# A two-layer graph network on one core: index tables kept in SBUF, a carry row fetched, vector features on ScalarE, a dense scale on GpSimd, four loads under way

## The chip, the cores and the metric

The kernel runs on one core of a Trainium2 chip. Its time is device microseconds (us) of one execution. The core's engines are TensorE (PE in the profile; PEld are its weight loads), VectorE (DVE), ScalarE (ACT), GpSimd (POOL) and SyncE (SP), and each works through its own queue of instructions in order. Semaphores tie the queues together.

## The reference

There are 100,000 nodes with 160 features (64 scalars, 32 vectors of three components) and 25,000 edges, sorted by destination. Two layers each normalise, send messages along the edges, sum them at the destination and add the result back:

```python
h = jnp.maximum(_layernorm(x), 0.0)
x = x + L0(h, node_vec1, edge_attr_4, edge_attr_8, ...)   # cos(angle) * self part + sin(angle) * edge part
h = jnp.maximum(_layernorm(x), 0.0)
x = x + L1(h, edge_attr_4, ...)                            # h + relu(linear(segment_sum(message)))
# L0, per edge, with gs, gv = linear(h)[src] and w1..w4 = silu(edge_attr_8 @ fc_w1) @ fc_w2:
m0a = gs * ys * w1;   m0b = sum(gv * yv, -1) * w4;   m1a = gs * yv * w2;   m1b = gv * ys * w3
mid = segment_sum([m0a, m0b, m1a, m1b], dst) / 4           # then two linear maps and the angle
```

A node without an incoming edge needs only its self part, and that is most of them.

## The kernel before, in words

Nodes are worked in 98 units of 1,024 (128 partitions by 8), edges in 196 tiles of 128, four tiles to a quad, so 49 quads (Q = 49, T = 196, GQ = 4). The program has four stages that follow one another.

**Head.** SP loads the tables of sources and destinations. DVE makes from them the gather index (`t_gat`), the scatter index (`t_put`: an edge that isn't the last of its destination gets an index out of range) and the keys `f_key` (own destination and that of the last edge before the tile). PE transposes the destinations into rows. SP stores all of these to DRAM by quad (lines 409 to 418). Then the edge network: for 13 groups of four quads, `net_load` brings the edge scalars, PE multiplies (`net_mm`, L1037), ACT applies SiLU (`net_silu`, L803), `net_store` writes the hidden values to DRAM.

**Stage 1** runs the dense part and the edge part of layer 0 together: 98 steps, each a unit of nodes and two tiles of edges (one half-step, or slot, for each tile). In a slot PE does the dense products of the unit before (`dense_mm`), transposes features of the tile before (`p1_feat_t`, L1090), then `p1_parts`, `p1_source` (the linear map of the gathered source rows and their weights, L1066), `p1_sum` (sum over equal destinations, L1078 and L1080) and `dense_tr` (L976). The sum and the dense transposes share PSUM bank 1, so `dense_tr` waits until ACT has copied the sum out (`p1_total`, L832, waited for as `e_tot`). ACT, in a slot: copy the transposed features (L838), the rest (L817), scale the source rows (`p1_source`, L824), copy the sum (L832), then the transposed dense rows (L795) and four layer-norm-and-relu instructions (`dense_h1`, L774). Two of the four slots of a quad differ: in one PE also transposes the next quad's edge rows, which ACT copies (L811) before PE may go on. DVE has the statistics, the dense residual (L1358), the features in three parts (L1423, L1428, L1432) and, each quad, two selector matrices (`selector`, L1384): `same` (edges of one destination) and `carry` (edges that continue the last destination of the tile before). POOL gathers the source rows by indirect DMA (`gather`, L606), makes scales, and adds `x1 + h1` (`dense_y`, L649).

**Stage 2** takes the destination rows again, quad by quad: POOL gathers four tiles (L606) and scatters four tiles of the layer's result (L612), index columns having been loaded by SP for each quad (`p2_index`, `p2_put`).

**Stage 3** is the edge part of layer 1, one tile to a slot. POOL alternates one scatter (L612) and one gather (L738), the gather seven tiles ahead. PE in slot n: transpose n-1, `p3_sum` n-4 (which waits for `m_sc`, the selectors), `p3_parts` n-2. DVE in slot n: features n, message n-2, output n-4, and in the last slot of a quad the selector `same` of the next quad (`p3_same`). SP, for each quad: `p3_load`, `p3_tables`, `p3_y`.

## Time and profile before

| | us |
|---|---|
| median of 3 runs (2452.57 to 2453.29) | 2452.86 |
| the profiled execution's own time | 2459.89 |
| its span, first to last instruction | 2458.1 |
| busy: PE / DVE / ACT / POOL | 1824.8 / 1873.4 / 1296.0 / 1477.5 |

The profiled execution is a single one, and took 7.0 us more than the median. Its span is what the views below divide up. Busy time is an average over four stages that differ, so a share of the whole says little about which engine a stage waits for.

### The profile page before, as it was taken

To read this page: it belongs to the slowest core of one execution; us is meant where nothing else is said; L and a number is where in the kernel's file an instruction comes from. 1 tells how busy PE (TensorE), PEld (TensorE's weight loads), DVE (VectorE), ACT (ScalarE), POOL (GpSimd) and SP (SyncE) were. 2 spreads that over 40 slices of the span, in tenths; PEclk is the share of its full clock that TensorE was granted. 3 is DMA by queue.
4 is the path that set the end of the run, shared out by engine and by line. 5 is a ranking of instruction groups with operands and counts; after the bars stand their busy time and mean duration, and the time that the engine had idled before them with its cause. 6 is when DMAs were issued, how large, how long until landed. Compare 5 with 4: busy or idle time off the path is not lost.

```text
span 2458.1 us, 51427 instructions
## 1 busy us (share of the span) xinstructions
PE 1824.8 (74%) x12730; PEld 1696.7 (69%) x12730; DVE 1873.4 (76%) x5982; ACT 1296.0 (53%) x3409; POOL 1477.5 (60%) x1432
## 2 busy tenths in 40 slices
PE   0788888888888888888888554544543788898887
PEld 0287778777787777877777544444443788888887
DVE  2099999999999999999999676666666566665564
ACT  0256666666666666666666555555555333333332
POOL 1045455554545555455553677777777777777776
PEclk9999999999999999999999755555555899998999
DMA  9445555555555555555555534334433334444443
GB/s 85 145 139 186 196 206 202 196 188 195 200 201 203 190 195 191 201 205 194 195 184 185 172 108 118 114 116 123 117 117 117 94 105 111 115 111 110 113 115 85
DMA packets 236558, 377.35 MB, mean 154 GB/s; under 512 B 116353, under 2 KB 146108, under 8 KB 236364
## 3 DMA queue, kind: packets, MB, share of 16 engines
q1 hardware_dynamic: 189484, 302.66, 39.1%
q0 software_dynamic: 47040, 74.31, 11.2%
q8 instruction: 12, 0.20, 0.0%
q14 instruction: 22, 0.18, 0.0%
HBM read 183.27 MB, written 201.21 MB: 156 GB/s over the span
## 4 chain that ended last, share of the span: by engine, by line
PE 33%; issue 17%; DVE 14%; ACT 12%; DMA 12%; POOL 6%; SPq 4%; ACTq 1%; DVEq 1%; POOLq 0%
ACT h L774 6%; PE bank L981 5%; DMA q_row<-row_tab 4%; PE bank L976 4%; DMA x_all<-in_xa,i_dst 3%; DVE st L1207 3%; POOL h_all L612 3%; PE bank L1090 3%; PE bank L982 3%; PE bank L1066 2%; DMA out<-yo,i_put 2%; POOL x_all L606 2%; PE bank L1158 2%; ACT h L889 2%; ACT tot L832 2%
## 5 line engine op out<-in xcount | busy, mean ns | idle before, releaser
L649 POOL TENSOR_TENSOR yo<-x,h 128x640 f32<-128x640 f32 x196 | 303.9, 1551 | 506.2 <-ACT h L774 504.9
L981 PE MATMUL bank<-wp,hT 128*128 128x160 f32 x1568 | 376.3, 322 | 0.0
L774 ACT ACTIVATE h<-x,nmr,inv 128x160 f32<-128x160 f32 x784 | 342.2, 514 | 1.5 <-DVE nmr L1211 1.5
L606 POOL DMA_INDIRECT x_e<-in_xa,i_src x192 | 210.8, 1098 | 161.1 <-issue 78.3
L981 PE MATMUL bank<-wp,eT 128*128 128x160 f32 x784 | 263.0, 428 | 51.2 <-ACT eR L897 43.7
L982 PE MATMUL bank<-wp,hR 128*128 128x64 f32 x1568 | 259.4, 247 | 0.0
L1358 DVE SCALAR_TENSOR_TENSOR x<-bank,scl,x_all 128x160 f32<-128x160 f32 x784 | 254.7, 365 | 5.1 <-PE bank L982 1.8
L982 PEld LDWEIGHTS bank<-wp,hR 128*128 128x128 f32 x1568 | 255.5, 190 | 0.0
L612 POOL DMA_INDIRECT out<-yo,i_put x196 | 209.7, 1070 | 74.3 <-issue 41.0
L612 POOL DMA_INDIRECT h_all<-h,i_put x196 | 217.4, 1109 | 59.8 <-issue 58.9
L976 PE MATMUL bank<-ident,h_e 128*128 128x128 f32 x392 | 83.9, 353 | 215.8 <-DVE hr_e L1527 215.4
L981 PEld LDWEIGHTS bank<-wp,hT 128*128 128x128 f32 x1568 | 237.7, 192 | 2.1
L738 POOL DMA_INDIRECT h<-h_all,i_src x196 | 200.2, 1022 | 61.5 <-issue 44.5
L606 POOL DMA_INDIRECT x_all<-in_xa,i_dst x196 | 192.4, 981 | 59.6 <-issue 57.8
L795 ACT ACTIVATE hT<-bank 128x512 f32<-128x512 f32 x196 | 117.0, 597 | 208.2 <-PE bank L977 208.2
L1207 DVE BATCH_NORM_STATS2 st<-x 128x6 f32<-128x320 f32 x490 | 217.9, 484 | 0.0
L976 PEld LDWEIGHTS bank<-ident,h_e 128*128 128x128 f32 x392 | 58.2, 185 | 224.7 <-DVE hr_e L1527 207.1
L981 PEld LDWEIGHTS bank<-wp,eT 128*128 128x128 f32 x784 | 163.5, 258 | 70.7 <-issue 38.2
L976 PE MATMUL bank<-ident,hb 128*128 128x128 f32 x784 | 124.3, 281 | 110.3 <-ACT tot L832 110.3
L946 ACT ACTIVATE tot<-bank 128x160 f32<-128x160 f32 x196 | 59.0, 301 | 267.9 <-PE bank L1181 264.0
L1158 PE MATMUL bank<-ident,feat 128*128 128x128 f32 x784 | 129.0, 290 | 93.2 <-DVE feat L1688 92.5
L976 PEld LDWEIGHTS bank<-ident,hb 128*128 128x128 f32 x784 | 83.1, 141 | 152.5 <-issue 137.6
(161 smaller groups left out, 5508.3 us busy)
## 6 DMA issues: line engine op xcount, KB each, us to landing
x_all<-in_xa SPq DMA_DIRECT2D x98, 644.0 KB, 5.0
h_all<-h SPq DMA_DIRECT2D x98, 640.0 KB, 3.0
out<-yo SPq DMA_DIRECT2D x98, 640.0 KB, 3.3
q_row<-row_tab SPq DMA_DIRECT2D x98, 256.0 KB
sum_tab<-tot SPq DMA_DIRECT2D x49, 322.0 KB, 4.2
y_tab<-yo SPq DMA_DIRECT2D x49, 320.0 KB
x<-y_tab SPq DMA_DIRECT2D x49, 320.0 KB
cv<-sum_tab SPq DMA_DIRECT2D x25, 322.0 KB, 3.2
```

The source lines that it names most:

```text
L606: nc.gpsimd.indirect_dma_start(into[:, t * width:(t + 1) * width], None, rows, bass.IndirectOffsetOnAxis(ap=index[:, t:t + 1], axis=0)).th ...
L612: nc.gpsimd.indirect_dma_start(rows, bass.IndirectOffsetOnAxis(ap=index[:, t:t + 1], axis=0), tile, None, bounds_check=N - 1, oob_is_err=F ...
L649: nc.gpsimd.tensor_tensor(yo[j][:, a:b], x1[j][:, a:b], h1[j][:, a:b], ALU.add).then_inc(d_y, 1)
L738: nc.gpsimd.indirect_dma_start(h1[j][:, t * D:(t + 1) * D], None, h1_all, bass.IndirectOffsetOnAxis(ap=i_src[j][:, t:t + 1], axis=0)).then ...
L774: ins = nc.scalar.activation(h1[j][:, k * D:(k + 1) * D], x1[j][:, k * D:(k + 1) * D], ACT.Relu, bias=nmr2[j][:, k:k + 1], scale=inv2[j][: ...
L795: nc.scalar.activation(hT[h][:, :], bank[0][:, :], ACT.Relu)
L976: nc.tensor.transpose(ps_main[:, t * P:(t + 1) * P], main[:, t * P:(t + 1) * P], ident[:, :])
L981: nc.tensor.matmul(dst_ps, main[:, t * P:(t + 1) * P], wp[:, w:w + D], start=True, stop=False)
L982: return nc.tensor.matmul(dst_ps[:, 0:DS], rest[:, :], wp[:, w + D + t * DS:w + D + (t + 1) * DS], start=False, stop=True)
L1158: ins = nc.tensor.transpose(bank[n.mod(2)][:, c * P:(c + 1) * P], feat[n.mod(2)][:, c * P:(c + 1) * P], ident[:, :])
L1207: return V.bn_stats(st[:, 2 * pair:2 * pair + 2, :].rearrange("p g k -> p (g k)"), two_rows[:, 0:D, :])
L1358: ins = V.scalar_tensor_tensor(x1[j][:, k * D:(k + 1) * D], bank[2 + pair % 2][:, k % 2 * D:(k % 2 + 1) * D], scl1[u.mod(4)][:, k:k + 1], ...
```

## The change

Five edits. (1) The index columns of a quad are copied on POOL from tables that stay in SBUF, into the small buffers that the indirect DMAs read. The four tables in DRAM, their stores and SP's loads of them go, and with them `q_key`; the selector `same` reads its keys from `f_dst` in SBUF, and the rows of destinations come from the host's transposed copy. (2) Of `carry` only the last partition holds anything: DVE makes all rows of it once in the head (`c_row`), they go to DRAM, and SP fetches one row for each quad into partition 127; the product that uses it contracts over 32 partitions. (3) The third part of the features (L1432) goes; ACT makes a second, scaled copy of the vector part of the source rows instead, three instructions of 32 columns for each tile, with a scale `scly` that POOL makes. (4) `dense_scale` moves from DVE to POOL. (5) The edge network has four loads under way, not two.

SP, head (stores that go) and the edge network:

```diff
-            sp.dma_start(src_tab.rearrange("q p c -> p q c"), t_src[:, :].rearrange("p (q c) -> p q c", c=GQ)).then_inc(s_tab_out, 16)
-            sp.dma_start(dst_tab.rearrange("q p c -> p q c"), t_gat[:, :].rearrange("p (q c) -> p q c", c=GQ)).then_inc(s_tab_out, 16)
-            sp.dma_start(put_tab.rearrange("q p c -> p q c"), t_put[:, :].rearrange("p (q c) -> p q c", c=GQ)).then_inc(s_tab_out, 16)
-            sp.dma_start(key_tab.rearrange("q p c -> p q c"), f_key[:, :, :]).then_inc(s_tab_out, 16)
...
-                wait(sp, n_mm, 2 * (g - 1))
...
+                wait(sp, n_mm, 2 * (g - 3))
...
-            net_load(0)
+            for g in range(4):
+                net_load(g)
+            sp.wait_ge(s_car, 1)
+            sp.dma_start(carry_tab[0:TA, :], c_row[0][0:TA, :]).then_inc(s_car_out, 16)
+            if T > P:
+                sp.dma_start(carry_tab[P:T, :], c_row[1][0:T - P, :]).then_inc(s_car_out, 16)
             for g in range(NB):
-                if g + 1 < NB:
-                    net_load(g + 1)
                 net_store(g)
+                if g + 4 < NB:
+                    net_load(g + 4)
```

SP's tables in stage 1, and in stage 3 (the waits come ahead of the loads):

```diff
             def p1_tables(q):
                 j = q.mod(2)
                 wait(sp, e_v, q.times(GQ, -GQ))
-                sp.dma_start(q_key[j][:, :], key_tab[q.times(1)]).then_inc(e_tb[j], 16)
                 sp.dma_start(q_ed[j][:, :], ed_q[q.times(1)]).then_inc(e_tb[j], 16)
                 sp.dma_start(q_row[j][:, :], row_q[q.times(1)].partition_broadcast(P)).then_inc(e_tb[j], 16)
+
+            def p1_carry(q):
+                j = q.mod(2)
+                wait(sp, e_seg, q.times(GQ, -GQ))
+                sp.dma_start(carry[j][P - 1:P, :], carry_q[q.times(1)].unsqueeze(0)).then_inc(e_ca[j], 16)
...
                 if v.within(U) and (v - 2).within(U):
                     x_load(v, last)
-                if v.mod(2) == 0 and (q + 1).within(Q):
-                    p1_load(q + 1)
+                if v.mod(2) == 0 and q.within(Q):
+                    p1_tables(q)
                 if v.mod(2) == 1 and q.within(Q):
-                    p1_tables(q)
+                    p1_carry(q)
                     p1_hidden(q)
...
             def p3_tables(q):
                 j = q.mod(2)
                 wait(sp, m_v, q.times(GQ, -GQ))
-                sp.dma_start(q_key[j][:, :], key_tab[q.times(1)]).then_inc(m_tb[j], 16)
+                wait(sp, m_seg, q.times(GQ, -GQ))
                 sp.dma_start(q_ed[j][:, :], ed_q[q.times(1)]).then_inc(m_tb[j], 16)
                 sp.dma_start(q_row[j][:, :], row_q[q.times(1)].partition_broadcast(P)).then_inc(m_tb[j], 16)
+                sp.dma_start(carry[j][P - 1:P, :], carry_q[q.times(1)].unsqueeze(0)).then_inc(m_tb[j], 16)
```

POOL:

```diff
+            for j in range(2):
+                nc.gpsimd.memset(carry[j][:, :], 0.0)
+            nc.gpsimd.memset(tot[1][:, :], 0.0).then_inc(s_cz, 1)
+
+            def index_copy(into, table, q, signal):
+                nc.gpsimd.tensor_copy(into[:, :], table[:, bass.ds(q.times(GQ), GQ)]).then_inc(signal, 1)
+                pool.wait_ge(signal, q.times(1, 1))
 
             def p1_gather(q):
                 j = q.mod(2)
-                pool.wait_ge(e_ix[j], q.over(2, 16, 16))
+                wait(pool, e_g[j], q.over(2, 64))
+                index_copy(i_src[j], t_src, q, e_ix)
                 wait(pool, e_cen, q.times(1, -1))
+                wait(pool, e_scl, q.times(4, -4))
                 gather(xa, x_e[j], XW, i_src[j], e_g[j])
...
+            def dense_scale(u):
+                j = u.mod(4)
+                pool.wait_ge(d_scl, u.times(2, 1))
+                nc.gpsimd.tensor_tensor(scl1[j][:, :], inv1[j][:, :], x3(x_in[j], XW, GD)[:, :, D], ALU.mult).then_inc(d_scl, 1)
...
+                pool.wait_ge(e_tb[j], q.over(2, 32, 32))
+                nc.gpsimd.tensor_tensor(scly[j][:, :].rearrange("p (t i) -> p t i", i=3), bc_last(scl_e[j][:, :], 3),
+                                        x3(q_ed[j], EW, GQ)[:, :, 1:4], ALU.mult).then_inc(e_scl, 1)
 
 
             def step(w):
                 q = At(w.i, w.c // 2, 2)
...
                 k = q.mod(4)
-                pool.wait_ge(r_ix[k], q.over(4, 16, 16))
+                wait(pool, r_g[k], q.over(4, 64))
+                index_copy(i_dst[k], t_gat, q, r_ix)
                 wait(pool, r_x1, q.times(2, -6))
                 gather(xa, x_q[k], XW, i_dst[k], r_g[k])
 
             def p2_scatter(q):
                 j = q.mod(2)
-                pool.wait_ge(r_px[j], q.over(2, 16, 16))
+                wait(pool, r_put[j], q.over(2, 64))
+                index_copy(i_put[j], t_put, q, r_px)
                 pool.wait_ge(r_h1, q.times(1, 1))
...
             def p3_gather(n):
                 j, t = n.c // GQ % 2, n.mod(4)
                 if t == 0:
-                    pool.wait_ge(m_ix[j], n.over(8, 16, 16))
+                    wait(pool, m_g[j], n.over(8, 64))
+                    index_copy(i_src[j], t_src, At(n.i, n.c // GQ, 2), m_ix)
...
                 if t == 0:
-                    pool.wait_ge(m_px[j], n.over(8, 16, 16))
+                    wait(pool, m_put[j], n.over(8, 64))
+                    index_copy(i_put[j], t_put, At(n.i, n.c // GQ, 2), m_px)
```

ACT in `p1_source`, PE in `p1_sum` and DVE's features and selector in stage 1:

```diff
+                act.wait_ge(e_scl, n.over(4, 4, 4))
                 wait(act, e_ft, n.times(1, -1))
-                nc.scalar.activation(g_e[n.mod(2)][:, :], bank[5 + n.mod(2)][:, 0:D], ACT.Copy,
-                                     scale=scl_e[j][:, t:t + 1]).then_inc(e_gg, 1)
+                g, b = g_e[n.mod(2)], bank[5 + n.mod(2)]
+                nc.scalar.activation(g[:, 0:D], b[:, 0:D], ACT.Copy, scale=scl_e[j][:, t:t + 1])
+                for c in range(3):
+                    ins = nc.scalar.activation(g[:, D + c:D + DV:3], b[:, DS + c:D:3], ACT.Copy,
+                                               scale=scly[j][:, 3 * t + c:3 * t + c + 1])
+                ins.then_inc(e_gg, 1)
...
-                before = tot[j][:, (t - 1) * CW:t * CW] if t else tot[1 - j][:, (GQ - 1) * CW:GQ * CW]
+                before = tot[j][P - 32:P, (t - 1) * CW:t * CW] if t else tot[1 - j][P - 32:P, (GQ - 1) * CW:GQ * CW]
                 nc.tensor.matmul(bank[1][:, U_SEG:U_SEG + CW], same[j][:, t * P:(t + 1) * P], v_e[n.mod(2)][:, :],
                                  start=True, stop=False)
-                nc.tensor.matmul(bank[1][:, U_SEG:U_SEG + CW], carry[j][:, t * P:(t + 1) * P], before,
+                nc.tensor.matmul(bank[1][:, U_SEG:U_SEG + CW], carry[j][P - 32:P, t * P:(t + 1) * P], before,
                                  start=False, stop=True).then_inc(e_seg, 1)
...
-                                       bc_last(q_key[j][:, key * GQ:(key + 1) * GQ], P), ALU.is_equal)
+            def selector(q):
+
+                j = q.mod(2)
+                key = f_dst[:, bass.ds(q.times(GQ), GQ)]
+                return V.tensor_tensor(x3(same[j], P, GQ), x3(q_row[j], P, GQ), bc_last(key, P), ALU.is_equal)
 
...
                     v.wait_ge(e_gg, n.times(1, 1))
                     wait(v, e_ftr, n.times(1, -1))
                     V.tensor_tensor(f[:, 128:320].rearrange("p (a u i) -> p a u i", a=2, i=3),
                                     w[:, 128:192].rearrange("p (a u) -> p a u", a=2).unsqueeze(3).to_broadcast([P, 2, DU, 3]),
-                                    g[:, DS:D].rearrange("p (u i) -> p u i", i=3).unsqueeze(1).to_broadcast([P, 2, DU, 3]),
-                                    ALU.mult).then_inc(e_fm, 1)
-                elif part == 1:
+                                    g[:, DS:D + DV].rearrange("p (a u i) -> p a u i", a=2, i=3), ALU.mult)
+                else:
                     V.tensor_tensor(f[:, 0:128].rearrange("p (a u) -> p a u", a=2), w[:, 0:128].rearrange("p (a u) -> p a u", a=2),
-                                    bc_mid(g[:, 0:DS], 2), ALU.mult)
-                else:
-                    v.wait_ge(e_fm, n.times(1, 1))
-                    V.tensor_tensor(f[:, 224:320].rearrange("p (u i) -> p u i", i=3),
-                                    f[:, 224:320].rearrange("p (u i) -> p u i", i=3),
-                                    bc_mid(ed(j, t, 1, 4), DU), ALU.mult).then_inc(e_ft, 1)
+                                    bc_mid(g[:, 0:DS], 2), ALU.mult).then_inc(e_ft, 1)
```

The order of instructions, at three places. POOL in the loop of stage 2, before: one gather of four tiles and one scatter of four, with SP's loads waited for.

```order
L72 ISA [waits p2_index_loaded0]
L606 DMA x_all<-in_xa,i_dst 128x161 [waits p2_x1_steps]
L606 DMA x_all<-in_xa,i_dst 128x161 x3
L703 ISA
L704 ISA [waits p2_put_loaded0]
L612 DMA h_all<-h,i_put 100000x160 [waits p2_h1_ready]
L612 DMA h_all<-h,i_put 100000x160 x3
L72 REGISTER_ALU [waits p2_index_loaded1]
L606 DMA x_all<-in_xa,i_dst 128x161 [waits p2_x1_steps]
L606 DMA x_all<-in_xa,i_dst 128x161 x3
```

The same place now (`i_dst` and `i_put` are the index columns of a quad):

```order
L620 ISA [waits p2_node_rows0]
L620 COPY i_dst<-t_gat 128x4
L621 ISA
L72 ISA [waits p2_index_copied]
L586 DMA x_all<-in_xa,i_dst 128x161 [waits p2_x1_steps]
L586 DMA x_all<-in_xa,i_dst 128x161 x3
L72 ISA
L620 ISA [waits p2_h1_scattered0]
L620 COPY i_put<-t_put 128x4
L621 ISA
L592 DMA h_all<-h,i_put 100000x160 [waits p2_put_copied,p2_h1_ready]
L592 DMA h_all<-h,i_put 100000x160 x3
```

Between two runs of four indirect DMAs there stands now a copy, and the DMA behind it waits for POOL's own copy.

ACT in a slot of stage 1, before:

```order
L817 ACTIVATE xr<-bank 128x65 [waits p1_message_ready]
L820 REGISTER_ALU
L822 ISA [waits p1_products_done]
L72 REGISTER_ALU [waits p1_scale_ready]
L824 ACTIVATE g_e<-bank,scl_e 128x160 [waits p1_features_ready]
L832 ACTIVATE tot<-bank 128x161 [waits p1_sum_done]
L72 ISA [waits dense_h_transposed]
L795 ACTIVATE hT<-bank 128x512 [waits dense_product_done]
L796 ACTIVATE hR<-bank 128x128
```

And now:

```order
L827 REGISTER_ALU [waits p1_products_done]
L72 REGISTER_ALU [waits p1_scale_ready]
L830 ACTIVATE g_e<-bank,scl_e 128x160 [waits p1_features_ready]
L832 ACTIVATE g_e<-bank,scly 128x32 x3
L841 ACTIVATE tot<-bank 128x161 [waits p1_sum_done]
L72 ISA [waits dense_h_transposed]
L800 ACTIVATE hT<-bank 128x512 [waits dense_product_done]
L801 ACTIVATE hR<-bank 128x128
```

Three more instructions stand between the source scale and the copy of the sum (`tot`), for which PE's next dense transposes wait.

SP in the loop of stage 3, one quad, before:

```order
L552 ISA [waits p3_h1_rows0]
L552 DMA i_src<-src_tab 128x4
L557 ISA [waits p3_message_ready]
L557 DMA q_key<-key_tab 128x8
L558 ISA
L558 DMA q_ed<-edges 128x24
L559 DMA q_row<-row_tab 128x512
L564 ISA [waits p3_out_ready]
L564 DMA x<-y_tab 128x640
L566 DMA i_put<-put_tab 128x4 [waits p3_out_scattered1]
```

And now:

```order
L542 ISA [waits p3_sum_done,p3_message_ready]
L542 DMA q_ed<-edges 128x24
L543 ISA
L543 DMA q_row<-row_tab 128x512
L544 DMA carry<-carry_tab 1x512
L549 ISA [waits p3_out_ready]
L549 DMA x<-y_tab 128x640
```

The load of the row tables waits now for `p3_sum_done` too, the sum of the last tile of the quad before, and the carry row is fetched last of three.

## Rows read from the trace of the kernel before

**Rows 1.** Stages 1 to 3: busy us of each engine, granted clock, DMA share.
```profile
core 0: us, PE busy (x) PEld busy (x) DVE busy (x) ACT busy (x) POOL busy (x), PEclk, DMA share, GB/s
118.00:1378.00 1260.00, 1049.75 (x8080) 987.84 (x8080) 1181.32 (x3324) 805.03 (x2251) 649.88 (x629) 1.00 0.55 193
1378.00:1908.00 530.00, 260.80 (x1029) 233.15 (x1029) 358.53 (x1523) 288.24 (x539) 408.87 (x392) 0.54 0.41 118
1908.00:2458.00 550.00, 464.99 (x3528) 457.70 (x3528) 319.06 (x1077) 184.19 (x588) 409.72 (x392) 0.93 0.40 107
```

**Rows 2.** Timeline of the head: start, length (us), engine, line, tile, idle before.
```profile
39.54 14.67 SPq L412 DMA_DIRECT2D key_tab<-f_key  x1
...
60.94 0.82 SPq L427 DMA_DIRECT2D yo<-scalars_t  x2
...
63.98 7.16 PE L1037 MATMUL bank<-yo,wp 32*128 32x512 f32 x8 [44.74 <-DMA yo<-scalars_t]
...
111.92 0.28 ACT L803 ACTIVATE x<-bank 128x128 f32<-128x128 f32 x1
```

**Rows 3.** DMA issues: the copy that the edge network waits for.
```profile
scalars_t<-in_scalars_t_in SPq DMA_DIRECT2D x1, 784.0 KB, 9.7
```

**Rows 4.** Timeline of PE in stage 1: the dense transposes of four slots.
```profile
603.50 0.63 PE L976 MATMUL bank<-ident,hb 128*128 128x128 f32 x4 [0.59 <-ACT tot L832]
...
609.18 0.63 PE L976 MATMUL bank<-ident,hb 128*128 128x128 f32 x4 [0.60 <-ACT tot L832]
...
615.92 0.63 PE L976 MATMUL bank<-ident,hb 128*128 128x128 f32 x4 [0.59 <-ACT tot L832]
...
623.37 0.63 PE L976 MATMUL bank<-ident,hb 128*128 128x128 f32 x4 [0.59 <-ACT tot L832]
```

**Rows 5.** Groups by line and shape: busy us, mean ns, idle before by releaser.
```profile
L795 ACT ACTIVATE hT<-bank 128x512 f32<-128x512 f32 x196 | 117.0, 597 | 208.2 <-PE bank L977 208.2
...
L1432 DVE TENSOR_TENSOR feat<-feat,q_ed 128x96 f32<-128x96 f32 x196 | 107.0, 546 | 0.0
...
L1090 PE MATMUL bank<-ident,feat 128*128 128x128 f32 x588 | 101.4, 282 | 87.5 <-ACT eR L812 47.3 <-DVE feat L1432 40.1
```

**Rows 6.** Timeline of ACT in stage 1, one slot.
```profile
608.08 0.39 ACT L824 ACTIVATE g_e<-bank,scl_e 128x160 f32<-128x160 f32 x1 [0.65 <-PE bank L1066]
608.62 0.30 ACT L832 ACTIVATE tot<-bank 128x161 f32<-128x161 f32 x1 [0.15 <-PE bank L1080]
...
610.69 1.75 ACT L774 ACTIVATE h<-x,nmr,inv 128x160 f32<-128x160 f32 x4
```

**Rows 7.** Groups by line: POOL's indirect DMAs of stages 2 and 3.
```profile
L612 POOL DMA_INDIRECT h_all<-h,i_put x196 | 217.4, 1109 | 59.8 <-issue 58.9 <-ACT h L889 0.3 <-DMA i_put<-put_tab 0.3
...
L612 POOL DMA_INDIRECT out<-yo,i_put x196 | 209.7, 1070 | 74.3 <-issue 41.0 <-DVE yo L1712 11.8 <-DVE feat L1688 10.8
L738 POOL DMA_INDIRECT h<-h_all,i_src x196 | 200.2, 1022 | 61.5 <-issue 44.5 <-DVE yo L1712 8.8 <-ACT feat L941 6.1
L606 POOL DMA_INDIRECT x_all<-in_xa,i_dst x196 | 192.4, 981 | 59.6 <-issue 57.8 <-ACT h L889 1.5 <-DMA i_dst<-dst_tab 0.3
```

**Rows 8.** Timeline of POOL in stage 1: a small instruction ahead of an indirect DMA.
```profile
285.48 0.20 POOL L669 TENSOR_TENSOR scl_e<-inv_e,x_e 128x4 f32<-128x4 f32 x1
286.41 1.08 POOL L606 DMA_INDIRECT x_e<-in_xa,i_src  x1 [0.73 <-issue]
287.79 0.95 POOL L606 DMA_INDIRECT x_e<-in_xa,i_src  x1 [0.30 <-issue]
...
312.14 1.07 POOL L606 DMA_INDIRECT x_e<-in_xa,i_src  x1 [0.96 <-issue]
```

**Rows 9.** Timeline of stage 3: a quad whose row table was asked for late.
```profile
1947.89 0.31 ACT L946 ACTIVATE tot<-bank 128x160 f32<-128x160 f32 x1 [1.23 <-PE bank L1181]
...
1949.92 0.33 SPq L559 DMA_DIRECT2D q_row<-row_tab  x1
...
1954.15 0.69 DVE L1384 TENSOR_TENSOR same<-q_row,q_key 128x512 f32<-128x512 f32 x1 [4.35 <-DMA q_row<-row_tab]
```

**Rows 10.** The stretch behind that wait, columns as in rows 1.
```profile
1954.00:1964.80 10.80, 9.25 (x59) 9.26 (x60) 6.03 (x21) 2.80 (x9) 7.68 (x8) 0.72 0.30 72
```

More of the change, by code:

```diff
@@ L192, in gnn_kernel @@
         i_dst = four("i_dst", [P, GQ], i32)
+        scly = two("scly", [P, 3 * GQ])
         i_put = two("i_put", [P, GQ], i32)
-        q_key = two("q_key", [P, 2 * GQ])
-        q_row = two("q_row", [P, GQ * P])
+        q_row = two("q_row", [P, GQ * P], i32)
         q_ed = two("q_ed", [P, GQ * EW])
@@ L211, in gnn_kernel @@
         tot = two("tot", [P, GQ * CW])
-        n_sct = [t[0:GQ * SW, 0:CH] for t in yo]
+        n_sct = [yo[i % 2][0:GQ * SW, i // 2 * CH:(i // 2 + 1) * CH] for i in range(4)]
         n_hid = [t[:, 0:GQ * 2 * P] for t in x1]
@@ L253, in gnn_kernel @@
         k_tab = sem("sorted_tables_loaded")
+        n_row = 64 if T > P else 32
         block = ctx.enter_context(nc.Block())
-        n_in = sem2("net_scalars_loaded")
+        n_in = [sem(f"net_scalars_loaded{i}") for i in range(4)]
         n_mm = sem("net_products_done")
@@ L302, in gnn_kernel @@
         e_st = sem2("p1_sum_stored")
[L303 to L306 removed]
+        r_ix = sem("p2_index_copied")
+        r_px = sem("p2_put_copied")
         r_cv = [sem(f"p2_sums_loaded{i}") for i in range(4)]
@@ L509, in _ @@
                 step(At(0, v), last=v == U - 1)
-            for q in range(4):
-                p2_index(At(0, q))
             step(At(0, U + 3), laststore=True)
@@ L531, in p2_step @@
             def p2_step(v):
-                if v.within(Q) and not At(v.i, v.c).within(4) or not isinstance(v.i, int):
-                    p2_index(v)
                 if (v - 1).within(Q):
                     p2_sums(v - 1)
-                if (v - 5).within(Q):
-                    p2_put(v - 5)
                 if (v - 6).within(Q):
@@ L1395, in p1_selectors @@
                 wait(v, e_seg, q.times(GQ, -GQ))
-                v.wait_ge(e_tb[q.mod(2)], q.over(2, 48, 48))
-                selector(same, q.mod(2), 0)
-                selector(carry, q.mod(2), 1).then_inc(e_sc, 1)
+                v.wait_ge(e_tb[q.mod(2)], q.over(2, 32, 32))
+                selector(q).then_inc(e_sc, 1)
             def p1_outer(n):
@@ L1718, in p3_same @@
                 v.wait_ge(m_tb[j], n.over(8, 48, 48))
-                selector(same, j, 0)
+                selector(At(n.i, n.c // GQ, 2)).then_inc(m_sc, 1)
             def p3_slot(n):
@@ L1731, in p3_slot @@
                     p3_same(n + 1)
-                if n.mod(4) == 0 and n.within(T):
-                    selector(carry, n.c // GQ % 2, 1).then_inc(m_sc, 1)
             p3_same(At(0, 0, 8))
```

199 lines of the change are left out of this document (81 added, 118 removed).

## The prediction

> **What bounds the kernel now.** I read the stages by their windows first, since the four stages have different limits [rows 1]. In stage 1 DVE is busy for 1181 of 1260 us and PE for 1050, so both are candidates. In stages 2 and 3 no engine seems full: POOL has 409 of 530 and 410 of 550. The groups of POOL's lines correct that [rows 7]. Every indirect DMA is preceded by about 0.30 us in which POOL waits for nothing that shows (59.8/196 and 59.6/196 in stage 2). A quad of stage 2 therefore costs POOL 4 x (1.109 + 0.305 + 0.981 + 0.304) = 10.8 us, and 49 of them 529 us: the whole stage. In stage 3 it is 4 x (1.070 + 0.30 + 1.022 + 0.30) = 10.8 again, 528 us, and 18 us of other waits (74.3 + 61.5 - 392 x 0.30). POOL is the bound of both stages, and anything put into its queue there is paid in full.
>
> For stage 1 I took the timeline of PE [rows 4]. Each dense transpose waits about 0.6 us for ACT's copy of the sum; the slots between them last 5.68, 6.74 and 7.45 us, and the fourth about 5.7 (a quad is 1260/49 = 25.7, [rows 1]). So PE and ACT form a loop: PE's sum, ACT's copy, PE's transposes. DVE reaches into it in one slot of four only: PE waits 40.1 us in all for DVE's last feature part (L1432), 0.8 us a quad, and 47.3 for ACT's `eR` [rows 5]. DVE is full but mostly not what PE waits for.
>
> In the head, SP issues table stores until it comes to the first loads of the edge network at 60.94; the one in [rows 2] takes 14.67 us of its queue. PE then works from 63.98, and the last SiLU ends at 112.2.
>
> **The change, part by part.**
>
> Head. The stores go. What is left ahead of the edge network is the copy of the scalars, which lands 9.7 us after its issue [rows 3]. SP issues it behind about a dozen other transfers of 0.3 to 0.8 us (lengths as the issues in [rows 2, 9]) and one more copy follows, so I put its landing at 21 to 22 us (an estimate), the first products at about 24.5: 39.5 us earlier than 63.98. The products themselves: eight passes span 7.16 us [rows 2], 0.89 each, and with loads always ready a little less; 48 long passes and the short last group make 42 to 43 us, against 47.9 (63.98 to 111.92). PE is the floor of this loop, so four loads under way save about 5. Head: -45 (from -38 to -50).
>
> Stage 1. DVE loses L1432 (107.0 us, [rows 5]), the `carry` selector (49 x about 0.69, as `same` in [rows 9]) and 98 small scales. That takes away the 0.8 us wait, and the long slot becomes as the first: 6.74 - 5.68 = 1.06 us a quad. Three instructions come onto ACT between the source scale and the copy of the sum. Their price has no row. From the 512-column copy (597 ns, [rows 5]) and the 161-column one (300 ns, [rows 6]) a column costs 0.846 ns, so 32 columns with a scale cost 390 - 128 x 0.846 = 280 ns, and one follows another 0.10 earlier than its end (four `h` of 514 ns, the mean of their group, in 1.75 us: 0.41 apart, [rows 6]). The scale then takes 0.29 + 3 x 0.184 = 0.84, the sum's copy starts at 608.92 and not 608.62: 0.30 late in each slot, 1.2 a quad. Net +0.14 a quad, +7 us. The bounds are 0 late (-52 us) and, without overlap, 0.39 + 3 x 0.28 = 1.23, 0.69 late (+83 us). The small scale moved to POOL, `scly` and the index copy of this stage lie in POOL's idle half (650 of 1260 busy, [rows 1]); were that cover gone, about 1.5 us a quad would show. SP's tables and carry row go out at least a slot before their use.
>
> How much DVE gains is also doubtful: L1432 has a mean of 546 ns at 96 columns, where `same` needs 690 for 512 columns, so most of it is waiting, and the removed instruction may only hand that wait on. The Trainium skill (GPSIMD Engine Reference, section 8, Key points) says that POOL shares its SBUF interfaces with VectorE and contends with DVE instructions that read two SBUF inputs; by it the wait moves to the next such instruction, a selector or the centring. The sum is the same by the one and by the other, as PE doesn't wait for DVE there.
>
> Stage 2. Two index copies a quad, 98 in all, on the engine that bounds the stage. No copy ahead of an indirect DMA stands in the trace here, but in stage 1 a four-column scale does [rows 8]: 0.20 long, then 0.73 (in other quads 0.96) before the DMA, against 0.30 between two DMAs, and the first DMA 1.08 against 0.95. So one copy costs 0.02 + 0.20 + 0.73 - 0.30 + 0.12 = 0.76 us (a small start gap of 0.02 taken). The least is 0.21, when the gap stays at 0.30; the most 1.0 with 0.96, as POOL here also waits for its own copy. The row is the nearest there can be, so I take 0.76: 98 x 0.76 = +74.5 us. SP's index loads that go were never waited for (0.3 us each, [rows 7]) and return nothing.
>
> Stage 3. The same 98 copies, POOL's quad becomes 12.3. Beside them there is a new wait. `p3_tables` now waits for the sum of the last tile of the quad before. That sum ends at 1947.87 in [rows 9], where ACT's copy starts. SP could issue `q_row` about 0.6 us later, after `q_ed`: 1948.5. In those rows it was issued at 1949.92 and DVE waited 4.35 us; issued 1.4 us earlier the wait is 2.9, and now in every quad. Behind it on DVE are `same`, then the next tile's features; PE's sum waits for `same`. PE is busy 465/49 = 9.5 us a quad, so its side of the stage becomes 9.5 + 2.9 to 3.3 (part of the selector) = 12.4 to 12.8. POOL's 12.3 and this run side by side and are coupled; I take 12.55, against 10.8: 49 x 1.75 = +86. The bounds are +20 (copy at 0.21, wait hidden) and +98 (12.8).
>
> Sum: -45 + 7 + 74.5 + 86 = +122.5. The profiled execution's own time is 2459.9, so 2582.4; the median of the runs was 7.0 lower: 2575.
>
> **Rivals.** What this kernel's measurement can tell from no change is about 0.2%.
>
> *Copies are nearly free.* POOL prepares the next DMA during the copy, 0.21 each: stage 2 +21, stage 3 +20 to +78. Total +3 to +81 us, 2456 to 2534. Against it: the gap of 0.73 behind a small instruction. 14%.
>
> *ACT's three instructions cost more.* Without overlap +83 in place of +7: 2651. The rows of `h` show overlap for long instructions, none shows it for short ones. The Trainium skill (ScalarE: Activation LUTs, Rules for kernel authors) budgets about 0.3 us for each ACTIVATE and 0.83 ns an element: by it the chain is 0.43 + 3 x 0.33 = 1.41 and the sum 0.87 late, estimated +119 for the stage. The four `h` at 0.41 agree with that budget (0.43), but they have two pointer operands where these have one. 10%.
>
> *The clock falls in stage 3.* After the late table the granted clock was 0.72 in the next 10.8 us [rows 10], between its levels of 1.2 and 2.4 GHz: 6.0 us at the lower, 3.0 us lost. PE had idled for the table. If each quad did so: 9.5 x 0.93 = 8.8 at full clock, + 2.9 + 3.0 = 14.7, +105 us over the forecast: 2680. For it: the idle comes in every quad. Against: it would be 2.9 to 3.3, not 4.35. 12%.
>
> *DVE was the bound of stage 1, so the kernel gets faster.* DVE is busy 12.05 us of a step of 12.86 [rows 1]. If a step shortens by all that DVE loses, 107 + 34 + 98 x 0.2 = 161 us: 2575 - 7 - 161 = 2407. It decides from 130 us in stage 1. Against: PE waits for ACT in every slot, and only 40.1 us for DVE. 11%.
>
> *The head doesn't shorten*, since the edge network still waits for something else: +45, 2620. 2%.
>
> **How the numbers follow.** My forecast has 51%, own range 2535 to 2625. 2475 to 2670 leaves out the faster case, the cheapest copies and the top of the clock case, under 2 in 10. Faster: 11% and a part of the cheap copies, 13%; within 0.2%, 3%; slower, 84%.
>
> **What will show it.** Head: the first product of L1037 near 24 us, stage 1 starting 40 to 50 us sooner. Stage 1: PE's dense transposes 5.9 to 6.0 us apart with no slot of 6.74, and 25.5 to 25.9 a quad; three `scly` rows of about 0.28 us. Stage 2: a row of the index copy of 0.2 us, the idle before the first of four DMAs near 0.7, 12.3 us a quad. Stage 3: DVE's `same` waiting about 3 us for `q_row` or `carry` in every quad, 12.3 to 12.8 a quad. The forecast is wrong if that idle is 0.3, or if stage 1 loses over 50 us.

## The result, and the profile after

The changed kernel takes 2707.57 us (median of 4 runs, 2697.84 to 2720.75), against 2452.73 of the kernel before in the same series (4 runs): a ratio of 1.104, with a 95% interval of 1.099 to 1.109. It is 10.4% slower, 133 us more than forecast. The profiled execution took 2703.2 us, its span is 2700.9.

The stages by their windows (columns as in [rows 1]):

```profile
73.00:1350.00 1277.00, 1083.26 (x8080) 991.22 (x8080) 1039.33 (x2981) 878.39 (x2839) 726.66 (x826) 1.00 0.55 191
1350.00:1955.00 605.00, 261.70 (x1029) 234.04 (x1029) 350.20 (x1518) 288.17 (x539) 420.11 (x481) 0.54 0.33 101
1955.00:2700.00 745.00, 631.27 (x3528) 541.17 (x3528) 292.46 (x1033) 183.63 (x589) 430.25 (x498) 0.81 0.29 80
```

Against [rows 1]: head -45 us, stage 1 +17, stage 2 +75, stage 3 +195. In stage 3 PE is busy for 631 us, 166 more with the same 3528 products, at a granted clock of 0.81 where it was 0.93.

To compare kernels I use from here on the time from the first to the last instruction of one line: of the dense residual in stage 1 (1237.3 us before, 1254.4 after), of `part` in stage 2 (499.3, 581.5), and of the second part of the features in stage 3 (526.8, 709.8; 48.75 quads, so 10.81 and 14.56 us a quad).

Groups by line of the changed kernel; they answer to [rows 5, 7] and to the wait in [rows 9]:

```profile
L1351 DVE SCALAR_TENSOR_TENSOR x<-bank,scl,x_all 128x160 f32<-128x160 f32 x784 | 255.8, 368 | 127.8 <-POOL yo L638 119.6 <-PE bank L991 4.9
L592 POOL DMA_INDIRECT h_all<-h,i_put x196 | 214.3, 1093 | 96.9 <-issue 50.4 <-POOL i_put L620 45.5 <-ACT h L898 1.0
L592 POOL DMA_INDIRECT out<-yo,i_put x196 | 198.9, 1015 | 215.3 <-DVE yo L1690 92.1 <-DVE feat L1666 78.2 <-issue 41.8
L586 POOL DMA_INDIRECT x_all<-in_xa,i_dst x196 | 194.6, 993 | 91.4 <-issue 46.2 <-POOL i_dst L620 42.4 <-DVE x L1571 2.8
L1378 DVE TENSOR_TENSOR same<-q_row,f_dst 128x512 f32<-128x512 int32 x98 | 67.6, 689 | 155.3 <-DMA carry<-carry_tab 107.9 <-DMA q_row<-row_tab 47.3
L643 POOL TENSOR_TENSOR scl<-inv,x_all 128x8 f32<-128x8 f32 x98 | 20.2, 206 | 244.1 <-DVE inv L1341 244.1
```

Three of them are as forecast: POOL waits for its own copy ahead of one DMA in four (45.5 and 42.4 us), and the selector waits 107.9 us for the carry row, 2.2 a quad. Two are new: VectorE waits 119.6 us for POOL's sum, and POOL 244.1 us for VectorE's inverse. And POOL waits for VectorE ahead of the scatters of stage 3 (92.1 + 78.2), so POOL isn't the bound there any more.

One thing of the text ahead of the prediction has to be set right. The sum that the tables of a quad now wait for is that of the quad before last, not of the quad before (`wait(sp, m_seg, q.times(GQ, -GQ))`). PE makes the sums four slots behind, so it comes in the last slot of the quad before, where VectorE wants to make `same`.

What is? Two slots of stage 3 in PE's timeline. First the last slot before a late table, with the clock full, then the same work 7.6 us later:

```profile
2301.46 0.33 SPq L543 DMA_DIRECT2D q_row<-row_tab  x1
2301.89 0.25 SPq L544 DMA_DIRECT2D carry<-carry_tab  x1
2301.94 0.60 PE L1162 MATMUL bank<-ident,feat 128*128 128x128 f32 x4
2302.37 0.44 PE L1184 MATMUL bank<-v_e,same 128*128 128x160 f32 x2
2302.74 0.54 PE L1185 MATMUL bank<-tot,carry 32*128 32x160 f32 x2
2303.21 0.41 PE L1170 MATMUL bank<-msg1s,fT 128*128 128x32 f32 x2
2303.45 0.52 PE L1171 MATMUL bank<-msg1a,fT 128*128 128x160 f32 x2
...
2304.72 0.69 DVE L1378 TENSOR_TENSOR same<-q_row,f_dst 128x512 f32<-128x512 int32 x1 [1.81 <-DMA carry<-carry_tab]
...
2306.04 0.66 PE L1162 MATMUL bank<-ident,feat 128*128 128x128 f32 x4 [1.39 <-DVE feat L1666]
...
2309.96 0.74 PE L1184 MATMUL bank<-v_e,same 128*128 128x160 f32 x2
2310.63 0.90 PE L1185 MATMUL bank<-tot,carry 32*128 32x160 f32 x2
2311.46 0.64 PE L1170 MATMUL bank<-msg1s,fT 128*128 128x32 f32 x2
```

The windows around the two:

```profile
2299.00:2304.00 5.00, 5.00 (x37) 4.31 (x37) 2.25 (x8) 1.75 (x7) 3.38 (x4) 1.00 0.35 97
2309.00:2314.00 5.00, 5.00 (x21) 4.34 (x21) 1.30 (x5) 0.94 (x3) 2.94 (x4) 0.50 0.15 46
```

Behind PE's idle of 1.39 us the granted clock is 0.50, its lower level of 1.2 GHz, and the same time holds 21 products and not 37. And even at the full clock the slot is long. Here is the same place in a kernel whose carry product contracts over all 128 rows (e5_all_three below):

```profile
2202.98 0.44 PE L1196 MATMUL bank<-v_e,same 128*128 128x160 f32 x2
2203.25 0.43 PE L1197 MATMUL bank<-tot,carry 128*128 128x160 f32 x2
2203.53 0.30 PE L1181 MATMUL bank<-msg1s,fT 128*128 128x32 f32 x2
2203.66 0.52 PE L1182 MATMUL bank<-msg1a,fT 128*128 128x160 f32 x2
```

From `same` to `msg1a` 0.68 us there, 1.08 here (2302.37 to 2303.45): the carry product starts 0.10 later, the next 0.19 later, and the one behind 0.11. That is 0.40 us a slot, around a product with a quarter of the rows. It isn't these two slots alone: over all slots of stage 3 that ran at the full clock the median is 1.08 us in the changed kernel (99 slots) and 0.69 in e5 (160).

### The profile page after: what moved, and what is told of

It is laid out like the page before. It is cut to its first block, busy times and chain, and to the rows that moved or that the text cites. A ratio compares the mean times of both kernels' runs of the same rounds, so it can differ in the third digit from the quotient of the medians.

```text
span 2700.9 us, 51701 instructions
## 1 busy us (share of the span) xinstructions
PE 2022.6 (75%) x12728; PEld 1786.0 (66%) x12728; DVE 1695.0 (63%) x5586; ACT 1368.6 (51%) x3997; POOL 1586.9 (59%) x1828
## 4 chain that ended last, share of the span: by engine, by line
PE 33%; POOL 25%; issue 24%; DMA 6%; ACT 5%; DVE 2%; SPq 2%; POOLq 1%; DVEq 0%; ACTq 0%
POOL x_all L586 6%; POOL h_all L592 6%; POOL yo L638 5%; DMA carry<-carry_tab 5%; PE bank L990 4%; POOL x_e L586 4%; PE bank L1162 4%; PE bank L1185 3%; PE bank L991 2%; PE bank L985 2%; PE bank L1184 2%; PE bank L1171 2%; ACT g_e L832 2%; PE bank L1170 2%; PE bank L1172 2%
## 5 line engine op out<-in xcount | busy, mean ns | idle before, releaser
L638 POOL TENSOR_TENSOR yo<-x,h 128x640 f32<-128x640 f32 x196 | 337.9, 1735 | 192.2 <-ACT h L779 186.8
L1351 DVE SCALAR_TENSOR_TENSOR x<-bank,scl,x_all 128x160 f32<-128x160 f32 x784 | 255.8, 368 | 127.8 <-POOL yo L638 119.6
L592 POOL DMA_INDIRECT out<-yo,i_put x196 | 198.9, 1015 | 215.3 <-DVE yo L1690 92.1
L586 POOL DMA_INDIRECT x_e<-in_xa,i_src x196 | 217.3, 1109 | 92.0 <-issue 47.7
L1675 DVE TENSOR_TENSOR xr<-bank,q_ed 128x96 f32<-128x96 f32 x196 | 50.2, 256 | 322.1 <-PE bank L1174 321.9
L1162 PE MATMUL bank<-ident,feat 128*128 128x128 f32 x784 | 150.7, 326 | 116.6 <-DVE feat L1666 116.5
```

What stands on the lines that cost most here:

```text
L586: nc.gpsimd.indirect_dma_start(into[:, t * width:(t + 1) * width], None, rows, bass.IndirectOffsetOnAxis(ap=index[:, t:t + 1], axis=0)).th ...
L592: nc.gpsimd.indirect_dma_start(rows, bass.IndirectOffsetOnAxis(ap=index[:, t:t + 1], axis=0), tile, None, bounds_check=N - 1, oob_is_err=F ...
L638: nc.gpsimd.tensor_tensor(yo[j][:, a:b], x1[j][:, a:b], h1[j][:, a:b], ALU.add).then_inc(d_y, 1)
L1162: ins = nc.tensor.transpose(bank[n.mod(2)][:, c * P:(c + 1) * P], feat[n.mod(2)][:, c * P:(c + 1) * P], ident[:, :])
L1351: ins = V.scalar_tensor_tensor(x1[j][:, k * D:(k + 1) * D], bank[2 + pair % 2][:, k % 2 * D:(k % 2 + 1) * D], scl1[u.mod(4)][:, k:k + 1], ...
```

## The experiments

Fourteen kernels, each timed in three rounds beside the kernel before (2454.6 to 2459.4 in the four series). Stage 3 has three separate costs, so I took them away one by one, in pairs and all together.

e1 lets the carry product contract over 128 rows again, in stage 3 (and alike in stage 1):

```diff
-                nc.tensor.matmul(b[:, 0:D], carry[j][P - 32:P, t * P:(t + 1) * P], before, start=False, stop=True).then_inc(m_seg, 1)
+                nc.tensor.matmul(b[:, 0:D], carry[j][:, t * P:(t + 1) * P], before, start=False, stop=True).then_inc(m_seg, 1)
```

e2 asks for the tables of stage 3 early and for the carry row apart, and PE waits for `m_ca` ahead of a quad's first sum:

```diff
                 wait(sp, m_v, q.times(GQ, -GQ))
-                wait(sp, m_seg, q.times(GQ, -GQ))
...
+            def p3_carry(q):
+                j = q.mod(2)
+                wait(sp, m_seg, q.times(GQ, -GQ))
+                sp.dma_start(carry[j][P - 1:P, :], carry_q[q.times(1)].unsqueeze(0)).then_inc(m_ca[j], 16)
```

e4 takes the four index copies of stages 2 and 3 off POOL, two to VectorE and two to ScalarE; the one of stage 2's gather:

```diff
-                wait(pool, r_g[k], q.over(4, 64))
-                index_copy(i_dst[k], t_gat, q, r_ix)
+                pool.wait_ge(r_ix, q.times(1, 1))
...
+            def index_ahead(q):
+                V.tensor_copy(i_dst[q.mod(4)][:, :], t_gat[:, bass.ds(q.times(GQ), GQ)]).then_inc(r_ix, 1)
```

**e1_full_rows, e2_carry_apart, e4_copies_elsewhere, e5_all_three** (one edit each, then the three together).

> The changed kernel, with the carry product of both edge stages contracting over all 128 partitions again (the other rows of carry are zero, so the sum is the same). Theory A: the 32-row product itself is dear. At full clock a slot of stage 3 lasts 2.56 us in the changed kernel against 2.17 before, and the 0.39 lie just around this product (0.10 ahead of it, 0.19 in it, 0.11 behind it), 1.6 us a quad or more at the lower clock: stage 3 loses 75 to 100 of its 745 us. In stage 1 the product is 0.27 us dearer a slot too, but ScalarE's three new instructions make the copy of the sum as late as that, so almost nothing comes back there (0 to -15). Total about 2620. Rival: PE is busier in stage 3 only because its clock is lower, and the row count costs nothing: no change, 2700 to 2710. Second rival: stage 1 gives 0.27 us a slot as well, 53 us: 2565.

> The changed kernel, with the edge and row tables of stage 3 asked for as early as before, and the carry row fetched apart behind the wait for the sums, on a semaphore of its own that PE waits for a slot or more later. Theory: the wait of 2.2 us a quad of VectorE for the carry row goes, the granted clock comes back to 0.93 or more as PE no longer idles for it, and POOL's quad with its two copies, 12.3 us, is the bound: stage 3 from 745 to about 605, total about 2565. Rival: the clock stays low (0.8) for another reason and only the wait goes: 13.0 us a quad, total about 2595. Rival: the wait was not what stood in the way: 2700.

> The changed kernel, with the index copies of stages 2 and 3 made by VectorE and ScalarE ahead of time instead of by POOL. Theory: stage 2 gives back its whole 75 us (605 to 530), since POOL is its bound; stage 3 gives back almost nothing (0 to -15), since there the late table, the 32-row product and the clock set 15.2 us a quad and POOL's 12.3 lie beside that. Total about 2625. Rival: POOL's copies are also part of stage 3's 15.2 us: 75 to 85 more, 2545.

> The three edits of the other runs together: full contraction, carry row apart, copies on VectorE and ScalarE. Theory: head as short as in the changed kernel (73 us), stage 1 about 1265 to 1277, stage 2 about 530, stage 3 again bound by POOL at 10.8 us a quad, 530 to 550, at a clock of 0.9 or more. Total 2400 to 2425, faster than before by 1 to 2 per cent. Rival: stage 1 is longer in the changed kernel by something else, and a further loss hides in stage 3: above 2460.

Measured: 2611.3, 2602.1, 2569.3 and 2425.1 us. e1 is as its theory; stage 1 stays at 1253.6, so the 32-row product costs nothing there. In e2 stage 3 is 605.6 us as expected, but my total was 37 us too low, and the total of the first rival (2595) is nearer: I had taken the 142 us off the window of 745, which also holds fill and tail; and the clock did not come back (0.87), as that rival said, which POOL's bound hides. e4 gave back stage 2 (505.0), and 63 us of stage 3 as well, where I expected none; its rival came nearer. e5 gives the whole loss of stage 3 back (516.5) and is 1.3% faster than the kernel before: ratio 0.987 (0.986 to 0.989).

**e10_late_only, e3_both, e12_rows_only** leave one cost each.

> The changed kernel with full contraction and the copies elsewhere, but with the late tables left: in stage 3 the late table stands alone. Theory: its chain (sum, SP, 3 us of transfers, selector, features, PE) sets the quad with or without POOL's copies: stage 3 (first to last feature) 590 to 620, near the 615.7 that it has with the copies; clock 0.88 to 0.92; total 2500 to 2530. Rival: POOL's copies made those 615.7 us, and alone the late table costs under 20: below 540, total under 2450. The kernel before with late tables had 654.8, but with one more load, of the keys, ahead of the row table.

> The changed kernel with full contraction and the carry row apart, POOL's index copies left in all stages. Theory: stage 3 is bound by POOL with its copies alone, 12.3 to 12.4 us a quad, 600 to 606 from first to last feature, as with the 32-row product (605.6): the product's 0.39 us a slot is hidden beside POOL. Total 2590 to 2600. Rival: PE's shorter slots also shorten POOL's waits: 570 to 590.

> The changed kernel with the carry row apart and the copies elsewhere, and the 32-row product left: of stage 3's three costs this one stands alone. Theory: it hides beside POOL (PE 10.3 us a quad at full clock, POOL 10.6 to 10.8), as in the kernel before, where it made stage 3 7 us shorter and the clock 0.99: stage 3 515 to 530, clock over 0.95, total 2422 to 2440. Rival: without the other two it still costs its 1.6 us a quad: 590, total 2500.

Measured: 2514.6, 2595.0 and 2423.6, each total as its theory; stage 3 of e12 is a little shorter than the 515 to 530 expected. Stage 3, first to last feature:

| 32 rows | late table | copies on POOL | kernel | us | a quad | clock |
|---|---|---|---|---|---|---|
| no | no | no | e5 | 516.5 | 10.59 | 0.94 |
| yes | no | no | e12 | 510.6 | 10.47 | 0.99 |
| no | yes | no | e10 | 606.6 | 12.44 | 0.90 |
| no | no | yes | e3 | 600.2 | 12.31 | 0.91 |
| yes | no | yes | e2 | 605.6 | 12.42 | 0.87 |
| no | yes | yes | e1 | 615.7 | 12.63 | 0.90 |
| yes | yes | no | e4 | 646.3 | 13.26 | 0.89 |
| yes | yes | yes | changed | 709.8 | 14.56 | 0.82 |

The late table and the copies lie side by side (12.44 and 12.31 make 12.63). The 32-row product alone costs nothing: PE's work grows to 10.3 us a quad and still fits beside POOL. On top of the other two it costs 94 us.

**b1_rows32, b2_late_tables** put one cost each into the kernel before.

> The kernel before, with one edit: the carry product of both edge stages contracts over the last 32 partitions (nothing else of the change). Theory: the 32-row product makes the sum end 0.27 us later in every slot of stage 1, and here no ScalarE instruction hides it, so stage 1 grows by up to 196 x 0.27 = 53 us; in stage 3 PE's four slots go from 2.17 to 2.56 us, 10.25 a quad and 0.5 to 1 of waits, just over POOL's 10.8: 0 to +25 us. Total 2455 + 53 + 12 = 2520 (2500 to 2535). Rival: the row count costs nothing and PE's slots in the changed kernel were long for another reason: 2455.

> The kernel before, with one edit: in stage 3 SP waits for the sums of the quad before last ahead of the key, edge and row tables, as in the changed kernel. Theory: the late table alone makes a chain through SP, the transfer, VectorE and PE that is longer than POOL's 10.8 us: about 12.0 to 12.6 a quad (the changed kernel with full rows had 12.63), +60 to +90 us in stage 3, and the granted clock there falls from 0.93 to 0.85 to 0.90. Total 2515 to 2545. Rival: the late table is hidden beside POOL as long as POOL has no copies, and only with them is it seen: under +15, 2470.

Measured: 2486.3 and 2586.9. b1 lies between its theory (2500 to 2535) and its rival: stage 1 grows by 28 us, not 53 (0.14 a slot), and stage 3 shrinks to 519.8 at a clock of 0.99. b2 is dearer than its theory (2515 to 2545): stage 3 takes 654.8, 128 us more, at 0.87. It issues one load more, of the keys, ahead of the row table than e10 does (606.6); that this is all of the difference wasn't tested.

**e13_filler** asks why the three add up to so much. It is the changed kernel with all its costs, and more work for PE:

```diff
+            def p3_fill():
+                for c in range(2):
+                    nc.tensor.matmul(bank[7][:, 0:384], wp[:, W_SC:W_SC + P], wp[:, 0:384], start=True, stop=True)
             def p3_slot(n):
+                if n.mod(4) == 1:
+                    p3_fill()
```

> The changed kernel, all three costs in place, with two products of 384 columns more for each quad of stage 3 (their result is read by nothing), at the place in PE's queue where it idles for the late table. Theory of the clock: PE's idle is what lets the clock fall to 1.2 GHz, and the low clock is 2.6 us of each quad's 14.56, so more work in that place makes the stage shorter: clock 0.95 or more, a quad near POOL's 12.3 to 12.9, stage 3 600 to 640 in place of 710, total 2600 to 2640. Rival: the clock falls for another reason (the 32-row product, the load of the chip), and the extra work, 1.3 us at full clock and 2.6 at the lower, is added in part: 710 to 770, total over 2700.

Measured: 2610.3 us. Stage 3 takes 608.4 us, 101 less with 100 large products more. The same 599 us of stage 3 in the changed kernel and in this one, by windows, the changed kernel first:

```profile
1973.00:2572.00 599.00, 526.37 (x2938) 451.34 (x2938) 243.38 (x860) 152.78 (x490) 352.38 (x410) 0.82 0.29 80
```

```profile
1973.00:2572.00 599.00, 560.25 (x3591) 454.68 (x3592) 282.80 (x993) 179.57 (x569) 411.00 (x472) 0.99 0.34 94
```

So it is PE's idle that lets the clock fall here, and the fallen clock is the amplifier: with it gone the quad is 12.48 us, near the 12.31 that POOL needs with its copies alone (e3).

The idle isn't all of it, though. Compare the changed kernel with e1, which differs from it by nothing but the rows of the carry product, over stage 3 of each:

```profile
1973.00:2683.00 710.00, 623.32 (x3478) 534.76 (x3478) 286.74 (x1017) 180.81 (x580) 412.29 (x477) 0.82 0.29 80
```

```profile
1976.00:2591.00 615.00, 488.46 (x3476) 480.66 (x3477) 285.24 (x1014) 181.38 (x579) 414.94 (x476) 0.90 0.33 92
```

In the changed kernel PE idles less (1.8 us a quad against 2.6), yet its clock is at the lower level for 256 us against 123, in 42 stretches against 36. So too with only one of the other two costs: 0.87 in e2 against 0.91 in e3, and 0.89 in e4 against 0.90 in e10, a smaller difference (147 us low against 119). With 32 rows the clock, once fallen, stays low longer; without idle, 32 rows leave it at 0.99 (e12, b1, e13). Why, no run here shows.

**e7_vector_features, e9_scale_only, e8_and_scale, e11_gather_first** are about stage 1. All start from e5. e7 takes ScalarE's three instructions and `scly` back, e9 the dense scale, e8 both; e11 is e7 with one swap in POOL's queue:

```diff
-                if (w - 1).within(U):
-                    dense_scale(w - 1)
                 if w.mod(2) == 0 and (q + 1).within(Q):
                     p1_gather(q + 1)
+                if (w - 1).within(U):
+                    dense_scale(w - 1)
```

> The changed kernel with full contraction, carry row apart and the copies elsewhere (2425 us), and the third part of the features back on VectorE in place of ScalarE's three instructions and POOL's small scale. Theory: ScalarE's three instructions hold the copy of the sum up by 0.26 us in each slot of stage 1 (51 us), and VectorE, with one selector less, no longer makes PE wait 0.8 us a quad: stage 1 goes from about 1277 to 1215 to 1225, total 2365 to 2375. Rival: VectorE's wait comes back in full, and the two nearly cancel: 2410 to 2420.

> The changed kernel with full contraction, carry row apart and the copies elsewhere (2425 us), and the small dense scale back on VectorE. Theory: POOL now waits for VectorE's inverse ahead of the gather and of x1 + h1, and VectorE later waits for POOL's sum (119.6 us in all in the changed kernel), but PE does not wait for VectorE there: stage 1 unchanged, 2420 to 2430, and VectorE's wait for POOL falls. Rival: this new ring between POOL and VectorE is what made stage 1 17 us longer: 2405 to 2412.

> The changed kernel with full contraction, carry row apart, copies elsewhere, and both the third part of the features and the small dense scale back on VectorE (what is left of the change is the short head, the carry row and the single selector). Theory: the ring that made stage 1 1378 us long with the features alone on VectorE is POOL's: its queue waits for VectorE's inverse ahead of the gather, the gather's 5 us lie ahead of x1 + h1, and VectorE waits for that. With the scale on VectorE there is no ring: stage 1 (first to last product of the residual) 1237 as before the change or up to 50 less, total 2365 to 2410, the fastest so far. Rival: VectorE is itself the bound with both on it (as in the 124 us of the run with the features alone): over 2500.

> The kernel with the features on VectorE (2555 us), with one edit: in POOL's queue the gather of a quad stands ahead of the small dense scale, so it no longer waits for VectorE's inverse. Theory of the ring: the gather starts up to 3 to 6 us earlier, x1 + h1 behind it comes in time, and at least 80 of the 124 us come back: 2420 to 2475. Rival: the load on VectorE is the cause and the place in POOL's queue makes nothing: 2550.

Measured: 2555.4, 2441.0, 2409.5 and 2488.5. Stage 1 (first to last residual product): e5 1253.7, e7 1377.9, e9 1262.2, e8 1237.1, e11 1318.5. e9 missed its theory and its rival, which both had it no longer than 2430: stage 1 grew by 8.5 us, and where the rest of the 16 us over e5 comes from I didn't find out. e7 was far off: I expected over 50 us less and got 124 more. Its timeline of POOL shows what stands in the way:

```profile
595.90 0.21 POOL L654 TENSOR_TENSOR scl<-inv,x_all 128x8 f32<-128x8 f32 x1 [3.03 <-DVE inv L1346]
596.08 0.18 POOL L631 COPY i_src<-t_src 128x4 int32 x1
597.25 1.42 POOL L595 DMA_INDIRECT x_e<-in_xa,i_src  x1 [0.98 <-POOL i_src L631]
...
602.45 3.04 POOL L649 TENSOR_TENSOR yo<-x,h 128x640 f32<-128x640 f32 x2
```

And its VectorE, meanwhile:

```profile
604.19 0.68 DVE L1356 SCALAR_TENSOR_TENSOR x<-bank,scl,x_all 128x160 f32<-128x160 f32 x2 [2.71 <-POOL yo L649]
```

The scale of 0.2 us waits for VectorE's inverse, with the gather and then the sum `x1 + h1` queued behind it; VectorE waits for that sum before the products that lead to its next inverse. That is a ring. With the gather ahead of the scale (e11, 2488.5 where I had 2420 to 2475) 59 of the 124 us come back, less than the 80 I had set; without the scale on POOL (e8) all do. So, with the features on VectorE, the scale's place on POOL is the cause, but the ring through the gather is only shown for those 59 us. For the rest there is a rival that no run separates: VectorE's centring (1024 columns) takes 1803 ns in the mean in e7 and 1862 in e11, against 1229 in e8, which is 56 and 62 us more over its 98 instructions. e8 is the fastest kernel here: ratio 0.982 (0.980 to 0.984). But its stage 1 is the 1237 of before and no better: VectorE still makes PE wait for its last feature part (29.8 us between 300 and 1200 us, 30.4 before), though it has one selector less.

## Why the prediction was wrong

*Head, forecast -45: right.* The first product stands at 24.04 us (forecast 24.5), the loop takes 42.2 (42 to 43), and the first residual product is at 83.1 where it was at 129.7: -46.6.

*Stage 1, forecast +7: measured +17, inside its bounds, with other reasons beside.* ScalarE's part came as forecast, in the timeline of the changed kernel:

```profile
607.65 0.39 ACT L830 ACTIVATE g_e<-bank,scl_e 128x160 f32<-128x160 f32 x1 [0.65 <-PE bank L1066]
607.94 0.65 ACT L832 ACTIVATE g_e<-bank,scly 128x32 f32<-128x32 f32 x3
608.45 0.32 ACT L841 ACTIVATE tot<-bank 128x161 f32<-128x161 f32 x1
```

The copy of the sum starts 0.80 us after the scale, 0.54 before [rows 6]: 0.26 late, forecast 0.30. PE's dense transposes stand 5.96, 5.98, 6.06 and 7.68 us apart (medians between 300 and 1200 us), so the slot of 6.74 is gone as forecast; a quad takes 25.81 us where it took 25.49, 0.32 more and not 0.14. The rival of dearer activates falls, and so does that of VectorE as the bound: its busy time in the stage fell from 1181 to 1039 us, and the stage grew. The sentence that puts the small scale into POOL's idle half was wrong in kind: POOL's idle half doesn't help, as the scale waits there with the gather and the sum behind it. It cost nothing in sight only because VectorE had been relieved (e5 against e9: the scale on POOL is worth 8.5 us; e7 against e8: it costs 141). On VectorE this scale had taken 645 ns in the mean, not the 0.2 us of the working. I named no queue behind that new wait. The other thing I missed, the 32-row product, hid behind ScalarE's lateness (e1), where it costs 28 us without it (b1).

On the doubt that the removed feature part would hand its waiting on, the trace agrees with the rule of the Trainium skill named there (GPSIMD Engine Reference, section 8, Key points): centring takes 1519 ns in the mean where it took 1228 (23 of the 98 take 2.40 to 2.57 us, the others 1.22 as before), and POOL's sum 1735 where it took 1551.

*Stage 2, forecast +74.5 from 0.76 us a copy: right* (the terms of that sum add up to 0.77). Without POOL's copies the stage is 581.5 - 505.0 = 76.5 us shorter, 0.78 each. The rest of the +82, some 6 us, is still there in all kernels without the copies (504.5 to 508.2, against 495.9 to 499.3 in the three with the stage as it was before). What makes it stays open.

*Stage 3, forecast +86: measured +183. This is the step that failed.* Its mechanisms are right, and so are their totals: the late table alone makes 12.44 us a quad (forecast 12.4 to 12.8), the copies alone 12.31 (12.3), both 12.63 (12.55). The first of these is right partly by luck: in e10 PE works 485.87 us of 606, 10.0 a quad, and idles 2.5, where the working had 9.5 and 2.9 to 3.3. What failed is the term "PE is busy 465/49 = 9.5 us a quad, so its side of the stage becomes 9.5 + 2.9 to 3.3": it took PE's work as unchanged, and it was 12.8. (The idle beside it was 1.8, less than the 2.9 to 3.3 of the working.)

First, the contraction over 32 rows, which I had described in the change, was given no price. It is 0.40 us a slot and 1.6 a quad. By the Trainium skill (TensorEngine Tiling, Key Properties) a change of tiling mode drains TensorE; the trace agrees, as the product itself starts 0.10 us later and the two behind it 0.19 and 0.11, though no run shows that it is this drain. Another page of the Trainium skill (TensorE: Matmul & The Clock Gate, Why this matters for your kernels) says that a single product with 32 rows takes as long as one with 128; here, between full ones, the next product starts 0.47 us behind it and not 0.28.

Second, the clock. PE's 12.79 us a quad (623.3/48.75) are 8.7 at full clock (four slots of 2.17, as in e5), 1.6 for the rows, and 2.5 for the low clock. By the windows it was low for 2 x (1 - 0.82) x 710 = 256 us, 5.2 a quad, and half of that, 2.6, is lost. PE's idle is another 1.8. Of the low clock 0.8 a quad was in the 9.5 already. So 9.5 + 1.6 for the rows + 1.8 more of low clock + 1.8 of idle = 14.7, measured 14.56. About half of the low clock goes with the rows, too: e1, without them, has 123 us of it and not 256.

The rival with 12%, "the clock falls in stage 3" (2680), named half of this and came nearest. That its 14.7 us a quad is so near the measured 14.56 is partly luck: it had no price for the rows, and 2.9 of idle where 1.8 were measured. Its counterargument, that an idle of 2.9 us is less than one of 4.35, had no row behind it; in this kernel an idle of 1.39 was enough. Without the 32 rows (e1) the kernel takes 2611 us, inside the 2535 to 2625 of the likeliest case; so that omission is what carried the time out of the range, by its own 1.6 us and by what the clock made of it. With the rows but without the fallen clock (e13) it takes 2610; neither carries it out without the other.

Of the 133 us over the forecast, stage 3 has 97, stage 1 10, stage 2 8 and the passages between the stages 7, less 2 from the head. The last 12 or so are no mechanism: the profiled execution of the kernel before was 7 us above its median, that of the changed kernel 4 below.

One sum of the rivals is off: with nearly free copies -45 + 7 + 21 + 78 is +61 us and not +81, so that case ends at 2514.

## What to carry to other kernels

Price every operand that changes shape, not only instructions added and removed: a product with fewer rows is not cheaper, and between full ones it is dearer. For a small instruction moved to an idle engine, ask what it waits for and what stands behind it in that queue; if the engine it waits for also needs what stands behind it, this is a ring. Don't add up costs of a stage with several near bounds: alone each of three was worth -6 to +90 us, together 193; and where PE idles and its clock falls, filling the idle shows within one run what the clock costs.
